# First attention: opening loads reordered, values' weights and output weights' rounding moved behind the first scores

## The reference, cut to what matters

```python
x = x + jnp.tanh(g_xattn[0]) * _L0_xattn_ref(_layernorm(x), ctx, ctx, mask, wq, wk, wv, wo, bq, bk, bv, bo)

def _L0_xattn_ref(query, key, value, mask, wq, wk, wv, wo, bq, bk, bv, bo):   # 16 heads of 32, 154 keys
    q = (query @ wq.T + bq); k = (key @ wk.T + bk); v = (value @ wv.T + bv)
    scores = clip(einsum('bhqd,bhkd->bhqk', q, k) * scale, -100, 100)
    scores = where(mask == 0, -inf, scores)
    out = softmax(scores) @ v
    return out @ wo.T + bo
```

## Time and profile before

| what | value |
|---|---|
| median of 3 runs | 2779.17 us (2778.12 to 2781.27) |
| the profiled execution | 2770.48 us |
| its span | 2768.7 us |
| TensorE matmul busy | 2552.4 us, 92% |
| VectorE busy | 1557.6 us, 56% |
| ScalarE busy | 1352.2 us, 49% |
| GpSimd busy | 1339.9 us, 48% |
| granted TensorE clock, mean | 0.971 |
| HBM read, written | 198.86 MB, 75.89 MB |

### The profile page before, as it was taken

One profiled execution on the slowest core, in us unless ns is written; L12 is line 12 of the kernel. 1 busy time (PEld: TensorE's weight loads), 2 busy tenths in 40 slices (PEclk: granted clock), 3 DMA queues, 4 the chain that ended last, 5 costly groups with the idle time before them and its releaser, 6 DMA issues. The chain is left out here.

```text
span 2768.7 us, 43616 instructions
## 1 busy us (share of the span) xinstructions
PE 2552.4 (92%) x16510; PEld 1357.6 (49%) x16510; DVE 1557.6 (56%) x2474; ACT 1352.2 (49%) x3019; POOL 1339.9 (48%) x1043
## 2 busy tenths in 40 slices
PE   6888889899999899999999978887999999999999
PEld 3333334344444377777777634443444444444444
DVE  6899977555555256565655567875643432334232
ACT  4788874222222166666666468876433222222221
POOL 4777770755555546676666448886102211121111
PEclk9999989999999999999999989998999999999999
DMA  7899995222221299999999769999410111011000
GB/s 208 164 202 182 188 170 185 62 62 62 62 62 46 86 315 283 282 290 287 282 275 290 179 149 188 200 185 202 134 39 16 46 46 34 13 46 46 23 8 31
DMA packets 587375, 389.75 MB, mean 141 GB/s; under 512 B 470048, under 2 KB 474912, under 8 KB 583200
## 3 DMA queue, kind: packets, MB, share of 16 engines
q1 hardware_dynamic: 550304, 319.64, 44.6%
q0 software_dynamic: 36864, 67.34, 11.8%
HBM read 198.86 MB, written 75.89 MB: 99 GB/s over the span
## 5 line engine op out<-in xcount | busy, mean ns | idle before, releaser
L1765 POOL DMA_INDIRECT ids<-sh_tk,sh_su x256 | 269.0, 1051 | 246.2 <-PE sh_gu L55 75.4
L2712 POOL TENSOR_TENSOR fe_prodT<-fe_pp,fe_prodT 128x512 f16<-128x512 f32 x64 | 77.8, 1215 | 590.9 <-ACT fe_prodT L2497 590.9
L55 PE MATMUL ex_gu<-ex_xT,ex_h 128*128 128x256 f16 x3072 | 347.4, 273 | 3.2 <-ACT ex_xT L2038 2.3
L2164 POOL DMA_INDIRECT xp<-ex_oo,ex_to x128 | 238.5, 1864 | 182.9 <-ACT ex_oo L2072 142.9
L55 PEld LDWEIGHTS ex_gu<-ex_xT,ex_h 128*128 128x128 f16 x3072 | 301.1, 98 | 52.6 <-ACT ex_xT L2038 2.6
L1899 DVE SCALAR_TENSOR_TENSOR ex_h<-ring,ex_h 128x1024 f16<-128x1024 f32 x128 | 151.2, 1222 | 158.7 <-ACT ex_h L1889 158.7
L55 PE MATMUL at_g<-hm_zT,hm_w 128*128 128x512 f16 x768 | 187.6, 399 | 14.8 <-DMA hm_zT<-hm_zs 11.7
L2628 DVE SCALAR_TENSOR_TENSOR ring<-fe_g,fe_nf,ring 128x512 f32<-128x512 f32 x32 | 24.0, 750 | 293.1 <-PE fe_g L2413 293.1
L1873 POOL DMA_INDIRECT ex_xg<-zrows,ex_idxu x128 | 157.0, 1226 | 57.2 <-issue 32.9
L55 PE MATMUL sh_g<-sh_wdn,sh_actT 128*128 128x512 f16 x768 | 174.6, 387 | 10.6 <-issue 6.9
L55 PE MATMUL ex_o<-ex_h,ex_aT 128*128 128x512 f16 x768 | 177.9, 382 | 0.0
(11 more groups left out here) (367 smaller groups left out, 5365.5 us busy)
## 6 DMA issues: line engine op xcount, KB each, us to landing
ring<-L_ffn_expert_gate_up_w SPq DMA_DIRECT2D x64, 1024.0 KB
ring<-L_ffn_expert_down_w SPq DMA_DIRECT2D x64, 512.0 KB
ring<-x SPq DMA_DIRECT2D x24, 1024.0 KB, 6.2
x<-ring SPq DMA_DIRECT2D x16, 1024.0 KB, 4.7
zrows<-hm_zs SPq DMA_DIRECT2D x32, 256.0 KB
xp<-ring SPq DMA_DIRECT2D x8, 1024.0 KB
out<-ring SPq DMA_DIRECT2D x8, 1024.0 KB, 4.3
ring<-xp SPq DMA_DIRECT2D x7, 1024.0 KB, 6.4
```

Source lines behind the costliest of these rows:

```text
L55: mm = nc.tensor.matmul(out, lhs(a, k), rhs(b, k), start=start and i == 0 and j == 0, stop=stop and i == n - 1 and j == 2)
L1765: e.indirect_dma_start(ids, bass.IndirectOffsetOnAxis(slotu[b % 2][:, t, j:j + 1], 0), pair[b % 2][:, t, j, :], None, bounds_check=SLOTS - ...
L2164: e.indirect_dma_start(dst, bass.IndirectOffsetOnAxis(to[:, n:n + 1], 0), o32[y % 2][:, t, :], None, bounds_check=T + SLOTS - 1, oob_is_er ...
L2712: e.tensor_tensor(prodT[:, 1, j, :], p32[q % 2][:, :], prodT[:, 0, j, :], ALU.subtract).then_inc(s["p_lo"], 1)
```

## The change

SyncE's opening becomes: context 0, bk, bq, the transposes of z as each tile is ready, mask 0, mask 1 (after lim_got), rows of block 2, rows of block 1, then wv, bo, bv, context 1 and wo. bq now counts on the keys' semaphore; the scaling of bo is a piece of its own on VectorE (at 0.5, behind the statistics of block 1 and ahead of values' rows 0.0). VectorE's memsets move from ahead of the opening to between the scaling of bq and the mask's steps. ScalarE rounds wq between tiles 1 and 2 instead of behind tile 3. wo is rounded at 2.2 instead of 0.3 (on ScalarE behind high(0), ahead of the exponentials of unit 1), and its low half made at 2.4 instead of 0.7 (on GpSimd behind rest 0).

```diff
--- before.py
+++ after.py
@@ -452,13 +452,16 @@
         for t in range(0, TPB, 2):
             opening += [("prepare", t), ("prepare", t + 1), ("low", t), ("low", t + 1)]
         opening += [("split", 0), ("keys", 0)] + [("turn", t) for t in range(TPB)]
-        opening += [("biases", 0), ("limits", 0), ("mask", 0), ("limits", 1), ("project", 0), ("project", 1)]
+        opening += [("first_mask", 0), ("biases", 0), ("blanks", 0), ("limits", 0), ("mask", 0), ("limits", 1), ("project", 0), ("project", 1)]
         for i, (what, k) in enumerate(opening):
             for engine in due:
-                at(engine, i - 100, what, 0, k)
+                early = engine == "scalar" and what == "split"
+                at(engine, opening.index(("prepare", 2)) - 100.5 if early else i - 100, what, 0, k)
+        at("vector", 0.5, "biases", 0, 1)
+        at("sync", -1.8, "weights_of_values", 0)
         at("sync", -1.5, "rest_of_weights", 0)
-        at("scalar", 0.3, "split", 1)
-        at("gpsimd", 0.7, "split", 1)
+        at("scalar", 2.2, "split", 1)
+        at("gpsimd", 2.4, "split", 1)
         for engine, later in (("tensor", (0.35, 1.35)), ("scalar", (1.2, 2.5))):
             for m, when in enumerate(later):
                 at(engine, when, "project", 0, 2 + m)
@@ -715,9 +718,11 @@
                     e.scalar_tensor_tensor(wq[:, 1, :, :], A.wq32[:, :, :], WS, wq[:, 0, :, :], ALU.mult, ALU.subtract
                                            ).then_inc(s["w_lo"], 1)
                 elif what == "biases":
-                    e.wait_ge(s["bias_in"], 48)
-                    e.tensor_scalar(bqs[:, :], bq[:, :], HD ** -0.5, None, ALU.mult)
-                    e.tensor_scalar(tbo[:, :], tbo[:, :], K.tg[:, 0:1], None, ALU.mult).then_inc(s["bias"], 1)
+                    if k == 0:
+                        e.tensor_scalar(bqs[:, :], bq[:, :], HD ** -0.5, None, ALU.mult).then_inc(s["bias"], 1)
+                    else:
+                        e.wait_ge(s["bias_in"], 32)
+                        e.tensor_scalar(tbo[:, :], tbo[:, :], K.tg[:, 0:1], None, ALU.mult).then_inc(s["bias"], 1)
                 elif what == "prepare":
                     if B == NB and k < 2:
                         e.wait_ge(s["lo"], TPB * NB - 1 + k)
@@ -725,6 +730,16 @@
                 elif what == "low":
                     if B == 0:
                         nm.vector_low(n)
+                elif what == "blanks":
+                    for g in range(BATCH):
+                        e.memset(VR[g][:, :, :, :], 0.0)
+                    e.memset(each[:, :], 1.0)
+                    e.memset(every[:, :], 0.0).then_inc(own, 1)
+                    e.wait_ge(own, next(step))
+                    for h in range(HG):
+                        ones = e.memset(every[HD * h:HD * h + HD, HD * h:HD * h + HD], 1.0)
+                    ones.then_inc(own, 1)
+                    e.wait_ge(own, next(step))
                 elif what == "limits":
                     l = lim[B % 2]
                     if k == 0:
@@ -808,19 +823,10 @@
                     e.wait_ge(s["k_mm"], KT * g + m + 1)
                     src_ = bank_of["k", g, m]
                     if g == 0 and m == 0:
-                        e.wait_ge(s["kbias_in"], 16)
+                        e.wait_ge(s["kbias_in"], 32)
                     o = e.tensor_scalar(KTn[g][:, m, :], src_[:, 0:CTX], bk[:, m:m + 1], None, ALU.add)
                     o.then_inc(s["k_out"], 1)
 
-            for g in range(BATCH):
-                e.memset(VR[g][:, :, :, :], 0.0)
-            e.memset(each[:, :], 1.0)
-            e.memset(every[:, :], 0.0).then_inc(own, 1)
-            e.wait_ge(own, next(step))
-            for h in range(HG):
-                ones = e.memset(every[HD * h:HD * h + HD, HD * h:HD * h + HD], 1.0)
-            ones.then_inc(own, 1)
-            e.wait_ge(own, next(step))
             for what in pieces_of("vector"):
                 piece(*what)
             e.wait_ge(s["x_out"], TPB * NB)
@@ -845,7 +851,7 @@
                     x = nrm.block(B)
                     e.wait_ge(s["z"], n + 1)
                     if n == 0:
-                        e.wait_ge(s["bias"], 1)
+                        e.wait_ge(s["bias"], 2)
                     e.tensor_tensor(x[:, k, :], x[:, k, :], tbo[:, :], ALU.add).then_inc(s["x_bias"], 1)
                 elif what == "split" and B:
                     e.wait_ge(s["w_hi"], 2)
@@ -875,6 +881,13 @@
             def piece(what, B, k):
                 if what == "turn_keys":
                     turn_keys(B, k)
+                elif what == "first_mask":
+                    mask(0)
+                elif what == "weights_of_values":
+                    A.sync_weights("wv")
+                    for to, n in ((tbo[:, :], "bo"), (bv, "bv")):
+                        e.dma_start(to, I[f"L0_xattn_{n}"].rearrange("(a n) -> a n", a=1).broadcast_to([P, D])
+                                    ).then_inc(s["bias_in"], 16)
                 elif what == "rest_of_weights":
                     A.sync_context(1, ctxb[1])
                     e.dma_start(A.x[3][:, :, :], A.weights_of("wo")).then_inc(s["wo_in"], 16)
@@ -923,13 +936,8 @@
 
             A.sync_context(0, ctxb[0])
             with nc.allow_non_contiguous_dma(reason="biases by head dim, once"):
-                for to, n, landed in ((bk, "bk", "kbias_in"), (bq, "bq", "bias_in")):
+                for to, n, landed in ((bk, "bk", "kbias_in"), (bq, "bq", "kbias_in")):
                     e.dma_start(to[:, :], I[f"L0_xattn_{n}"].rearrange("(k p) -> p k", p=P)).then_inc(s[landed], 16)
-            mask(0)
-            A.sync_weights("wv")
-            for to, n in ((tbo[:, :], "bo"), (bv, "bv")):
-                e.dma_start(to, I[f"L0_xattn_{n}"].rearrange("(a n) -> a n", a=1).broadcast_to([P, D])
-                            ).then_inc(s["bias_in"], 16)
             for what in pieces_of("sync"):
                 piece(*what)
 
```

## The result

On the same chips, 12 runs of each, the kernel before took 2781.77 us in the median (2778.12 to 2789.09) and the changed one 2789.62 us (2784.85 to 2795.98). The ratio is 1.0032 with a 95% interval of 1.0021 to 1.0044, so it is slower by 8.9 us (5.8 to 12.2). The prediction had + 5.0 us and 2784.2 us, in a range of 2775 to 2788: the sign is right, the size too small, and the measured median lies 1.6 us above the top of the range. Part of that distance is the base: the prediction added its sum to the median of 3 runs, 2779.17 us, and with nine more runs the same kernel's median is 2781.77, 2.6 us higher. As a difference of medians, 7.9 us were measured against 5.0.

The account below looks back on a forecast made before the run. It took the first attention's engines, handing units on in fixed order, to have no room for a late start. Late wv + 2.1 and wo's rounding + 2.9 gave + 5.0 us on the median 2779.17: 2784.2 us, range 2775 to 2788.

Parts of the forecast that it names:

- The opening up to the first scores: First attention's start: earlier transposes and projection 0 at full clock bring first scores at 28.05 instead of 33.60, 5.5 us earlier.
- The queue behind lim_got: SyncE's loads behind the second mask's wait: they start at 24.3 instead of 24.08, 0.2 us later, with DMA engines idle before.
- wv at 35.6: Values' weights, one load behind block 1's rows, land at 35.6; TensorE has nothing to do from 28.8 until then.
- The rival that wv comes at 37.05: Loads behind the wait go at the first burst's pace: wv + 3.6, total + 6.5 or 2785.7 us; chance 0.20.
- The low clock at + 1.53: TensorE at values' rows after 6.8 us idle: 1.53 us lost, as charged for 4.09 us idle; second clip + 2.1.
- wo's rounding, + 2.9 of wait: ScalarE's 3.85 us of rounding ahead of the second unit's exponentials, less 0.94 slack, makes VectorE's high(1) 2.9 us late.
- GpSimd's low part of wo ... nothing more: GpSimd's 4.08 us on wo's low half ends at about 58.0, just when block 1's low halves are due; no cost.
- The shift carried to the end: A shift at about 60 us, here + 5.0, travels through the fixed order of engines as a shift of the whole.
- The rounding is hidden: Rival: VectorE late enough at high(1) that the rounding's 2.9 us go, leaving + 2.1, 2781.3 us; chance 0.12.
- the opening's gain lives: Rival: wv at 32.5 and clock up, second clip 2.5 us earlier; at most the full - 5.5, 2773.7 us; chance 0.13.

Follow-up runs that it names:

- cut1 pair: Kernel before and changed kernel, both cut off behind the first attention, with plain DMAs for the transposing ones; medians 437.67 and 445.70 us.
- full_after: Changed kernel with all stages, only the transposing DMAs replaced by plain ones and a small logarithm bias; median 2782.32 us.
- cut1_after: Changed kernel cut off behind the first attention, with plain DMAs for the transposing ones; median 445.70 us.
- cut3_after: cut1_after once more, as second base on the chip of cut3_best; median of 5 runs 447.34 us.
- cut1_low: cut1_after with only GpSimd's low half of wo moved from 2.4 to 3.1, behind rest(1); median 444.63 us.
- cut1_round: Kernel before, cut with plain DMAs, with only wo's rounding moved to 2.2 and its low half to 2.4; median 442.58 us.
- cut2_lead: cut1_after with block 1's rows, wv, bo and bv right behind the first mask, then block 2's rows, second mask behind them all; median 439.93 us.
- cut3_before: Kernel before cut off behind the first attention, with plain DMAs, as base on the chip of cut3_best; median of 5 runs 438.00 us.
- full_before: Kernel before with all stages, only the transposing DMAs replaced by plain ones and a small logarithm bias; median 2770.02 us.
- cut3_best: cut1_after with wv, bo, bv, block 1's rows, wo and block 2's rows ahead of the second mask, wo's rounding at its old place; median 433.51 us.

## Why the prediction was wrong, by its own steps

- **The opening up to the first scores: right.** Transposes no longer behind the loads, projection 0 right behind the keys at full clock. 5.5 us earlier had been predicted; the cut1 pair, which starts alike, shows 5.9. In the changed kernel VectorE's list began at 7.22 instead of the 8.20 that I had taken, so its 6.8 hold up to a microsecond of an earlier start. Against a base that opened at full clock it is 4.0 and 4.5.
- **The queue behind lim_got: right.** The last mask's issue ended at 23.89; 24.3 had been named for its start. It is the mechanism that turns 6 us won into 2 lost, and it was there to be read: SyncE's queue, served in order, stood still at its wait, and the DMA engines moved nothing from 22 to 24 us.
- **wv at 35.6: right.** 34.25 in the changed kernel and 34.45 in full_after; 35.18, 35.70 and 36.10 in cut1_after, cut3_after and cut1_low. The rival that wv comes at 37.05 did not happen.
- **The low clock at + 1.53: too small.** 8 matmuls took 5.90 to 6.30 (6.19 in the changed kernel) instead of 3.70, 2.2 to 2.6 us more, after idle times of 6.6 to 7.0; the prediction charged what 4.09 us had cost. (That was itself 1.69, not 1.53: at full clock the 24 matmuls take 5.34, not twice 2.75.) wv's earlier landing cancelled it: + 2.1 us at the second clip had been predicted, + 2.15 in the cut1 pair and + 1.6 in the two kernels were measured. That is luck in the size, and luck in the base too: against the other kind of base the same change shows + 3.0 and + 3.45 at the third clip. The sum took one execution's low clock as a property of the kernel before.
- **wo's rounding, + 2.9 of wait: right.** 2.75 in the changed kernel, 2.74 or 2.75 in cut1_after, cut1_round, cut1_low and cut2_lead.
- **"GpSimd's low part of wo ... nothing more": wrong, the step that failed.** I asked when it would be through and who needs its result (block 1's low halves), and not what it runs beside. It runs beside VectorE's casts, which cannot run with it, and pushes the bias addition into the second of them: + 1.76 in the changed kernel, 1.75 in cut1_round with the loads untouched. Before the change it ran beside the second clip, which reads the scores out of PSUM, and that took its 1.43 us as ever; a row that made the low part look free. In the executions in which the kernel before opens 1.5 us or more earlier it was not free either (z took 2.56 in cut3_before and 1.50 in full_before instead of 0.99). The Trainium skill's rule above would have priced it: by it, as an estimate, the cast has to wait for what is left of the 4.08; in the changed kernel that was 57.56 - 56.53 = 1.03 us for the first.
- **The shift carried to the end: right for the loss, and the sum short.** 2.15 + 2.74 + 1.75 = 6.6 at the 4th clip, + 6.75 measured in the cut1 pair, and 7.57 and 8.03 in the pairs whose base opened at full clock. The cut kernels end 8.0 and 9.3 later and the whole 8.9 (5.8 to 12.2). So of what the sum of 5.0 lacks, 1.75 is the casts, up to 1.4 is the base's opening, and what arises behind the 4th clip, 1 to 2 us, was not isolated.
- **The range.** Its top had been worked out from wv being later and a second stretch of low clock. It held no term for the stretched casts, because the step had been costed at nothing without a bound. With 0 to 4.08 us, the length of the GpSimd instruction, as the bound, the range would have held the result. The 1.6 us above its top are also less than the 2.6 by which the base's median moved when nine runs were added.
- **The rivals.** "The rounding is hidden" and "the opening's gain lives" both fell. cut2_lead shows why the second falls even with wv in time: the rounding and the casts beside its low part take 4.6.

## What to carry to other kernels

When a piece is moved, ask of each of its instructions what will run beside it and whether the two can run together, also where nobody waits for its result; a cost of nothing needs a bound too. In a queue served in order, loads that wait for nothing belong ahead of the one that waits, and those that the next engine in line needs first ahead of the others. A wait that is removed is worth only its distance to the next one: here wv, then block 1's rows, then the rounding of wo had to be dealt with before the 3.7 us won at the first clip (cut3_best against cut3_before) could show at the fourth clip (3.95) and at the end of the stage (4.5 in the medians). And profile the base more than once: two executions of one kernel can differ by more than the term that is being priced.

## What the runs showed of the hardware that I had not expected

VectorE's f32 to f16 cast from SBUF does not run beside GpSimd's `tensor_tensor`: 0.26 us alone, 4.12 beside one of 4.05 us, and 1.33 beside one of 1.26; and GpSimd waits for the cast in its turn (six additions in 9.85 us instead of 7.56). The `tensor_scalar` that makes z behaves alike (0.99 alone, 1.93 with 1.2 us of GpSimd's instruction left). The clip that reads PSUM does not (1.43 us inside GpSimd's 40.96 to 45.04). After 6.6 to 7.0 us of idle time TensorE's first work ran at a granted clock of 0.50 and lost 2.2 to 2.6 us (in the changed kernel the clock is 0.50 from 36 to 38 us and 0.67 from 38 to 40, with work since 34.25). And the same kernel can fall to 0.50 in one execution and not in the next: its first 24 matmuls took 7.03 us behind 4.09 to 4.38 us of idle time and 5.34 behind 3.41 and 3.49.
